# A graph layer's edge network: the constant row of its second layer as two 64-row matmuls, and six gather buffers with a wait every third unit

## The chip, the cores and the metric

The kernel runs on one core of a Trainium2 chip. The metric is the device time of one execution in microseconds (us), taken as the median of several runs. Next to it stands one execution recorded by the hardware profiler; every duration below comes from that one.

## What is computed

One layer of a graph network over 6250 nodes with 256 features and 206250 edges, sorted by destination. Cut to what matters:

```python
h = maximum(layernorm(x), 0)
e = relu(raw @ W_e1.T + b_e1) @ W_e2.T + b_e2        # raw: 64 features of an edge
edge_emb = e * (clip(polarity, 0, 1) + 0.01) @ W_le.T + b_le
msg = relu(h[src] + edge_emb)
aggr = segment_sum(msg, dst, num_segments=6250)
g = (h + aggr) @ W_g1.T + b_g1
out = x + relu(layernorm_affine(g)) @ W_g2.T + b_g2
```

The product of W_e2 and W_le is formed once, so that the edge network has two layers: 64 to 256 with a rectifier, then 256 to 256. The second layer's constant row, c2 = b_e2 @ W_le.T, is added by a matmul of its own.

## The kernel before

The program has three parts, each with lists of instructions written by hand for every engine and joined by semaphores.

**prepare** normalises the nodes and writes h + b_le to a gather table in HBM, while VectorE also splits the weights into a high and a low half (fp32r numbers, of which two stand for one fp32). `fuse` (lines 165 to 176) forms the weights' product and c2; `vector` (from line 184) copies c2 and splits it into rows 0 (high) and 32 (low) of the otherwise zero tile `c2r` (lines 239 to 243). At its end VectorE computes the low halves of the first three units' edge features (`raw_low`, line 405).

**edge_path** goes through 403 units of 512 edges. For unit u:

- GpSimd (lines 530 to 539) issues four indirect DMAs of 128 rows each, which gather h[src] into `hx`, a ring of NX = 4 units. From unit 4 on it waits ahead of each unit's four until VectorE has added the rows of unit u-4 (semaphore `r_t`).
- TensorE has, in this order, the first layer of unit u+1 (lines 675 and 676, four matmuls of 512 columns), the second layer of unit u (lines 685 to 692), and the segment sum of unit u-1 (line 704, four matmuls). Every seventh unit two transposes follow (line 711). The second layer works in two halves q, each in a PSUM bank of its own out of four (`LB`): one matmul of 512 columns with the all-ones tile `onr` and c2, over all 128 array rows (line 685), then twelve of 256 columns.
- ScalarE makes the high halves of the hidden layer (548) and of the messages (554), the one-hot matrices of the destinations (563, 570) and the high half of the features of unit u+3 (400).
- VectorE has, in this order, the low half of the hidden layer of unit u+1 (line 604), for each of four groups of 128 edges the product with the gate plus the gathered row (line 615, in place in the PSUM bank), the low half of the features of unit u+3 (line 405, which reads two tiles of SBUF), and the low half of the messages (line 625). Its wait for a gather stands ahead of each line 615.

Ahead of its second layer TensorE waits for both halves of the hidden layer of unit u; ahead of each bank's first matmul it waits for the low half of the messages of unit u-2 in that bank (`r_ml`).

**node_update** then runs the two last products over the nodes. A fourth part for inputs with crowded destinations exists and is skipped at run time with these inputs.

Of the kernel before, what the change touches and what calls it, by code (L numbers as in the profile page):

```python
# [13 lines left out]
D = 256  # L14
F = 64
# [13 lines left out]
GE = GU * 4 * P  # L29
TOP = NP - P  # L30
NR = 3
NX = 4
NM = 4
AHEAD = 5
FUSE = 8
# [6 lines left out]
def gnn(nc, x, src, dst, src_m, dst_m, pol_m, pol, first, attrT, W_e1T, b_e1, b_e1r, W_e2, b_e2, W_leT, b_le,  # L42
        W_g1T, b_g1, ln_g, ln_b, W_g2T, b_g2, out):
    ctx = ExitStack()
    with ctx:
# [25 lines left out]
        flag_i = sb("flag_i", [1, 1], I32)  # L71
        b1 = sb("b1", [P, 2])
        wc = sb("wc", [P, 2, D])
        c2 = sb("c2", [1, D])
        ble = sb("ble", [P, D])
        lng = sb("lng", [P, 2])
        lnb = sb("lnb", [P, 2])
# [6 lines left out]
        def setup(c):  # L84
# [82 lines left out]
            def fuse(eng):  # L167
                eng.wait_ge(s_w, 16 * len(loads))
                for k in range(2):
                    for m in range(2):  # L170
                        eng.matmul(bank[0][:, D * k:D * k + D], we2[:, m, P * k:P * k + P], wle[:, m, :],
                                   start=(m == 0), stop=(m == 1))
                for m in range(2):
                    last = eng.matmul(bank[1][0:1, 0:D], be2[:, m:m + 1], wle[:, m, :],
                                      start=(m == 0), stop=(m == 1))
                last.then_inc(s_c, 1)

# [5 lines left out]
            def vector(eng):  # L183
                n = [0]

                def link(ins):
                    n[0] += 1
                    ins.then_inc(s_v, 1)
                    eng.wait_ge(s_v, n[0])

                w = 4 * GU
                m = FULL // w
                sv = slot[:, 0:m * w].rearrange("p (g k) -> p g k", k=w)
                bv = base[:, 0:m].rearrange("p (g k) -> p g k", k=1).broadcast_to([P, m, w])
                eng.wait_ge(s_io, 1)
                eng.tensor_copy(iota[:, :], iota_i[:, :])
                eng.memset(low2[:, :], 0.0)
                yield
                eng.wait_ge(s_i, 16 * len(edges))
                eng.tensor_copy(base[:, :], first_i[:, :])  # L200
                link(eng.tensor_copy(slot[:, :], dst_i[:, :]))
                link(eng.tensor_scalar(base[:, :], base[:, :], float(TOP), None, ALU.min))
                yield
                eng.tensor_copy(base_i[:, :], base[0:1, :])
                eng.tensor_tensor(sv, bv, sv, ALU.subtract)
                link(eng.tensor_scalar(slot[:, m * w:TILES], slot[:, m * w:TILES], -1.0, base[:, m:m + 1],
                                       ALU.mult, ALU.add))
                yield
                eng.tensor_reduce(low2[:, 0:1], slot[:, 0:FULL], axis=AX.X, op=ALU.max)
                yield  # L210
                eng.tensor_reduce(low2[:, 1:2], slot[:, 0:FULL], axis=AX.X, op=ALU.min)
                yield
                eng.tensor_copy(low2[0:TAIL, 2:3], slot[0:TAIL, FULL:TILES])
                link(eng.tensor_copy(low2[0:TAIL, 3:4], slot[0:TAIL, FULL:TILES]))
                link(eng.tensor_scalar(low2[:, 0:4:2], low2[:, 0:4:2], 0.0, None, ALU.is_gt))
                link(eng.tensor_scalar(low2[:, 1:4:2], low2[:, 1:4:2], float(1 - P), None, ALU.is_lt))
                eng.tensor_reduce(bad[:, 0:1], low2[:, :], axis=AX.X, op=ALU.max).then_inc(s_bad, 1)
                yield
                eng.wait_ge(s_w, 16 * len(loads))
                eng.wait_ge(s_m, 5)  # L220
                eng.tensor_copy(g1r[0:1, :], bg1[:, :])
                eng.tensor_copy(wgr[:, 0, :, :], wg1[:, :, :])
                link(eng.tensor_copy(wgr[:, 2, :, :], wg2[:, :, :]))
                yield
                eng.tensor_tensor(g1r[32:33, :], bg1[:, :], g1r[0:1, :].bitcast(F32), ALU.subtract)
                eng.tensor_tensor(wgr[:, 1, :, :], wg1[:, :, :], wgr[:, 0, :, :].bitcast(F32), ALU.subtract)
                yield
                eng.tensor_tensor(wgr[:, 3, :, :], wg2[:, :, :], wgr[:, 2, :, :].bitcast(F32), ALU.subtract)
                eng.tensor_copy(w1r[0:F, 0, :], w1[0:F, :])
                eng.tensor_copy(w1r[F:P, 1, :], w1[F:P, :])  # L230
                link(eng.tensor_copy(w1r[0:1, 1, :], btmp[0:1, :]))
                yield
                link(eng.tensor_copy(btmr[32:33, :], btmp[32:33, :]))
                eng.tensor_tensor(w1r[F:P, 0, :], w1[F:P, :], w1r[F:P, 1, :].bitcast(F32), ALU.subtract)
                eng.tensor_tensor(w1r[32:33, 1, :], btmp[32:33, :], btmr[32:33, :].bitcast(F32), ALU.subtract)
                yield
                eng.wait_ge(s_c, 1)
                link(eng.tensor_copy(wc[:, :, :], bank[0][:, :].rearrange("p (k n) -> p k n", k=2)))
                link(eng.tensor_copy(c2[:, :], bank[1][0:1, 0:D]))
                yield  # L240
                eng.tensor_copy(c2r[0:1, :], c2[:, :])
                link(eng.tensor_copy(wcr[:, 0, :, :], wc[:, :, :]))
                eng.tensor_tensor(c2r[32:33, :], c2[:, :], c2r[0:1, :].bitcast(F32), ALU.subtract)
                eng.tensor_tensor(wcr[:, 1, :, :], wc[:, :, :], wcr[:, 0, :, :].bitcast(F32), ALU.subtract)
                yield
                eng.wait_ge(s_f, 1)
                eng.tensor_copy(flag_i[:, :], bank[2][0:1, 0:1])
                yield
# [1 line left out]
            return {"weights": weights, "indices": indices, "gpsimd": gpsimd, "gates": gates, "fuse": fuse, "count_bad": count_bad,  # L250
                    "vector": vector}

        def nodes(c, tag, s_o):
            x_sb = sb(f"x_sb{tag}", [P, NT, D], F32, c)
            h = sb(f"h{tag}", [P, 2, 4, D], F32, c)
            nb = sb(f"nb{tag}", [P, NT], F32, c)
            G = len(NODE_GROUPS)
            s_z = sem(f"s_z{tag}", c)
            s_bl = sem(f"s_bl{tag}", c)
            s_x = [sem(f"s_x{tag}_{i}", c) for i in range(G)]  # L260
            s_st = sem(f"s_st{tag}", c)
            s_ag = sem(f"s_ag{tag}", c)
            s_ep = sem(f"s_ep{tag}", c)
# [27 lines left out]
            def vector(eng):  # L291
                eng.memset(x_sb[96:P, NT - 1, :], 0.0).then_inc(s_z, 1)
                for s in range(G + 1):
                    if s < G:
                        t, n = NODE_GROUPS[s]
                        eng.wait_ge(s_x[s], 16)
                        for k in range(t, t + n):
                            last = eng.bn_stats(st[:, k, :], x_sb[:, k, :])
                        last.then_inc(s_st, 1)
                        eng.wait_ge(s_st, s + 1)  # L300
                        for k in range(t, t + n):
                            last = eng.bn_aggr(mv[:, k, :], st[:, k, :])
                        last.then_inc(s_ag, 1)
                        eng.wait_ge(s_ag, s + 1)
                        eng.tensor_scalar(rs[:, t:t + n], mv[:, t:t + n, 1], EPS, None, ALU.add).then_inc(s_ep, 1)
                    if s >= 1:
                        t, n = NODE_GROUPS[s - 1]
                        eng.wait_ge(s_sq, s)
                        eng.reciprocal(rs[:, t:t + n], rs[:, t:t + n]).then_inc(s_rs, 1)
                        eng.wait_ge(s_rs, s)  # L310
                        eng.scalar_tensor_tensor(out=nb[:, t:t + n], in0=mv[:, t:t + n, 0], scalar=-1.0,
                                                 in1=rs[:, t:t + n], op0=ALU.mult, op1=ALU.mult).then_inc(s_n, 1)
                    yield s
# [93 lines left out]

        def prepare():
            with ExitStack() as c:  # L409
                b = nodes(c, "a", s_oa)  # L410
                a = setup(c)
                block = c.enter_context(nc.Block())

# [44 lines left out]
        def nodes_again():  # L458
            with ExitStack() as c:
                s_ob = sem("s_ob", c)  # L460
                b = nodes(c, "b", s_ob)
                block = c.enter_context(nc.Block())

                @block.sync
# [26 lines left out]
        def edge_path():  # L491
            with ExitStack() as c:
# [37 lines left out]
                def _(eng):  # L530
                    eng.wait_ge(s_oa, 16 * len(NODE_GROUPS))
                    for u in range(UNITS):
                        if u >= NX:
                            eng.wait_ge(r_t, 2 * (u - NX) + 2)
                        for j in range(4):
                            t = 4 * u + j
                            eng.indirect_dma_start(out=hx[:, u % NX, j, :], out_offset=None, in_=tables,  # L537
# [127 lines left out]
                def _(eng):  # L665
# [13 lines left out]
                    def second_layer(u):  # L679
                        eng.wait_ge(r_hh, 2 * u + 2)  # L680
                        eng.wait_ge(r_hl, 2 * u + 2)
                        for q in range(2):
                            if u >= 2:
                                eng.wait_ge(r_ml, 2 * (u - 2) + q + 1)
                            eng.matmul(LB[(2 * u + q) % 4][:, :], onr[:, :], c2w, start=True, stop=False)  # L685
                            for j in range(2):
                                o = LB[(2 * u + q) % 4][:, D * j:D * j + D]
                                e0 = (2 * q + j) * P
# [39 lines left out]
        def general_path(tag):  # L728
            with ExitStack() as c:
# [62 lines left out]
                with nc.Fori(0, NS) as i:  # L792
# [13 lines left out]
                    with nc.Block() as block:  # L806
# [21 lines left out]
                        def _(eng):  # L828
# [4 lines left out]
                            eng.wait_ge(s_hid, 1)  # L833
                            for k in range(2):
                                eng.matmul(bank[2][0:ST, 0:D], hid[:, k, :], wc[:, k, :], start=(k == 0), stop=False)
                            eng.matmul(bank[2][0:ST, 0:D], ones[0:1, 0:ST], c2[:, :], start=False, stop=True).then_inc(s_l2, 1)
                            eng.wait_ge(s_ms, 1)
                            eng.matmul(bank[3][0:ST, 0:D], eq[:, :], msr[:, :], start=True, stop=True).then_inc(s_sum, 1)

# [333 lines left out]
```

## Time and profile before

| | |
|---|---|
| median of 3 runs | 2294.32 us (2292.06 to 2301.87) |
| the profiled execution | 2291.79 us |
| its span, first to last instruction | 2290.1 us |
| TensorE matmul busy | 2220.2 us (97%) |
| VectorE busy | 2143.2 us (94%) |
| ScalarE busy | 1881.2 us (82%) |
| GpSimd busy | 1706.5 us (75%) |
| mean granted TensorE clock | 0.991 |

The span is 1.7 us shorter than the execution. Busy shares are means over stages: prepare lasts to about 72 us, the edge stage to about 2174 us, the node update to the end. GpSimd's busy time leaves out the time between the issue of one gather and the next. Matmuls are pipelined, so that the duration of one reaches beyond the start of the next; the distance from start to start is what one costs in a stream.

### The profile page before, as it was taken

The numbers are of one execution on the slowest core, as the hardware profiler recorded it, in microseconds if no ns is written. First come the engines' busy times: TensorE is split into PE (matmuls) and PEld (weight loads), VectorE is DVE, ScalarE is ACT, GpSimd is POOL, SyncE is SP. The second block draws the span as 40 slices with busy tenths as digits, with TensorE's granted clock in tenths as the row PEclk, the third lists the DMA queues.
The fourth block names the chain that finished last, engine by engine and source line by source line (L and its number), as shares of the span: only waits on it lengthen the run. The fifth ranks groups of instructions, "written<-read, shape, count | busy, mean of one in ns | idle before, by whom it ended". The sixth has DMA issues, their size and how long they took to land. (4 is left out here: it accounts for less than half of the span.)

```text
span 2290.1 us, 45615 instructions
## 1 busy us (share of the span) xinstructions
PE 2220.2 (97%) x14665; PEld 2021.1 (88%) x14665; DVE 2143.2 (94%) x4129; ACT 1881.2 (82%) x4267; POOL 1706.5 (75%) x1671
## 2 busy tenths in 40 slices
PE   3899999999999999999999999999999999999988
PEld 3799999999999999999999999999999999999887
DVE  8899999999999999999999999999999999999888
ACT  6788888888888888888888888888888888888754
POOL 7677777777777777777777777777777777777672
PEclk9899999999999999999999999999999999999989
DMA  9466666666666666666666666666666666666342
GB/s 301 133 158 151 154 152 153 152 153 152 153 152 154 152 153 153 153 153 152 154 151 153 152 152 153 154 152 155 150 154 151 156 150 155 151 153 152 99 132 95
DMA packets 138613, 349.58 MB, mean 153 GB/s; under 512 B 34113, under 2 KB 60674, under 8 KB 138370
## 3 DMA queue, kind: packets, MB, share of 16 engines
q0 software_dynamic: 77376, 211.39, 34.6%
q1 hardware_dynamic: 60994, 135.21, 24.9%
q8 instruction: 121, 1.98, 0.4%
q14 instruction: 122, 1.00, 0.2%
HBM read 333.64 MB, written 12.82 MB: 151 GB/s over the span
## 5 line engine op out<-in xcount | busy, mean ns | idle before, releaser
L537 POOL DMA_INDIRECT hx<-gather_table,sidx x1612 | 1601.7, 994 | 498.5 <-issue 474.1
L691 PE MATMUL bank<-wcr,hh 128*128 128x256 f32 x3224 | 904.6, 281 | 0.0
L690 PE MATMUL bank<-wcr,hh 128*128 128x256 f32 x3224 | 903.3, 280 | 0.0
L692 PE MATMUL bank<-wcr,hl 128*128 128x256 f32 x3224 | 903.2, 280 | 0.0
L615 DVE SCALAR_TENSOR_TENSOR bank<-bank,gt,hx 128x256 f32<-128x256 f32 x1612 | 698.9, 484 | 88.7 <-PE bank L692 86.4
L554 ACT ACTIVATE mhl<-bank 128x512 fp32r<-128x512 f32 x806 | 483.1, 599 | 308.1 <-PE bank L704 187.5
L691 PEld LDWEIGHTS bank<-wcr,hh 128*128 128x128 f32 x3224 | 606.3, 188 | 36.8
L690 PEld LDWEIGHTS bank<-wcr,hh 128*128 128x128 f32 x3224 | 609.2, 189 | 18.1
L692 PEld LDWEIGHTS bank<-wcr,hl 128*128 128x128 f32 x3224 | 605.9, 188 | 0.0
L625 DVE SCALAR_TENSOR_TENSOR mhl<-bank,mhl 128x512 fp32r<-128x512 f32 x806 | 519.2, 686 | 12.6
L604 DVE SCALAR_TENSOR_TENSOR hl<-bank,hh 128x512 fp32r<-128x512 f32 x806 | 514.8, 679 | 4.4 <-ACT hh L548 4.1
L563 ACT ACTIVATE away<-iota,slot 128x128 f32<-128x128 f32 x1612 | 518.1, 401 | 0.0
L548 ACT ACTIVATE hh<-bank 128x512 fp32r<-128x512 f32 x806 | 437.7, 598 | 14.6 <-PE bank L676 8.4
L704 PE MATMUL bank<-mhl,oh 128*128 128x512 f32 x1612 | 443.0, 396 | 1.5 <-DVE mhl L625 1.5
L675 PE MATMUL bank<-rhi,w1r 128*128 128x512 f32 x806 | 322.8, 400 | 7.7 <-PEq L409 7.0
L676 PE MATMUL bank<-rlo,w1r 128*128 128x512 f32 x806 | 320.5, 398 | 0.0
L685 PE MATMUL bank<-c2r,onr 128*128 128x512 f32 x806 | 319.4, 396 | 0.0
L704 PEld LDWEIGHTS bank<-mhl,oh 128*128 128x128 f32 x1612 | 273.1, 188 | 39.9 <-DVE mhl L625 1.9
L405 DVE TENSOR_TENSOR rlo<-raw,rhi 64x512 fp32r<-64x512 f32 x403 | 277.8, 690 | 12.6
L570 ACT ACTIVATE oh<-away 128x512 fp32r<-128x512 f32 x403 | 256.7, 637 | 0.0
L400 ACT CAST rhi<-raw 128x512 fp32r<-128x512 f32 x403 | 250.9, 623 | 0.0
L675 PEld LDWEIGHTS bank<-rhi,w1r 128*128 128x128 f32 x806 | 151.6, 188 | 42.8 <-DVE rlo L405 7.1
(112 smaller groups left out, 1173.4 us busy)
## 6 DMA issues: line engine op xcount, KB each, us to landing
raw<-in_attrT SPq DMA_DIRECT2D x402, 256.0 KB, 4.7
hx<-gather_table,sidx POOLq DMA_INDIRECT x1612, 2.9
x_sba<-in_x SPq DMA_DIRECT2D x12, 512.0 KB, 9.6
gather_table<-x_sba SPq DMA_DIRECT2D x12, 512.0 KB, 6.8
u_x<-in_x SPq DMA_DIRECT2D x12, 512.0 KB, 8.7
out<-u_x SPq DMA_DIRECT2D x12, 512.0 KB
dst_i<-in_dst_m SPq DMA_DIRECT2D x1, 805.5 KB
sidx<-in_src_m SPq DMA_DIRECT2D x1, 805.5 KB
```

The lines of the kernel that those rows point to most:

```text
L537: eng.indirect_dma_start(out=hx[:, u % NX, j, :], out_offset=None, in_=tables, in_offset=bass.IndirectOffsetOnAxis(ap=sidx[:, t:t + 1], ax ...
L548: eng.activation(hh[:, u % 2, k, :], LA[k][:, :], ACT.Relu).then_inc(r_hh, 1)
L554: eng.activation(mh[:, u % 2, 2 * q:2 * q + 2, :], LB[(2 * u + q) % 4][:, :].rearrange("p (j n) -> p j n", j=2), ACT.Relu).then_inc(r_mh, 1)
L563: last = eng.activation(away[:, u % 2, j, :], iota[:, :], ACT.Abs, bias=slot[:, t:t + 1])
L604: eng.scalar_tensor_tensor(out=hl[:, u % 2, k, :], in0=LA[k][:, :], scalar=0.0, in1=hh[:, u % 2, k, :].bitcast(F32), op0=ALU.max, op1=ALU. ...
L615: last = eng.scalar_tensor_tensor(out=b, in0=b, scalar=gt[:, t:t + 1], in1=hx[:, u % NX, 2 * q + j, :], op0=ALU.mult, op1=ALU.add)
L625: eng.scalar_tensor_tensor(out=ml[:, u % 2, 2 * q:2 * q + 2, :], in0=LB[(2 * u + q) % 4][:, :].rearrange("p (j n) -> p j n", j=2), scalar=0.0,
L675: eng.matmul(LA[k][:, :], w1r[:, 0, k * P:k * P + P], rhi[:, u % NM, :], start=True, stop=False)
L690: eng.matmul(o, hh[:, u % 2, k, e0:e0 + P], wcr[:, 0, k, :], start=False, stop=False)
L691: eng.matmul(o, hh[:, u % 2, k, e0:e0 + P], wcr[:, 1, k, :], start=False, stop=False)
L692: last = eng.matmul(o, hl[:, u % 2, k, e0:e0 + P], wcr[:, 0, k, :], start=False, stop=(j == 1 and k == 1))
L704: last = eng.matmul(SG[g % 2][:, :], oh[:, u % 3, j, :], mhl[:, u % 2, j, :, :], start=(u % GU == 0 and j == 0), stop=(ends and j == 3))
```

## The change

c2 is formed in all 128 rows of its tile, and `c2r` holds its halves twice, in rows 0 and 32 and in rows 64 and 96. The constant row of half q is then added by a matmul over array rows 64q to 64q + 63 alone; the two stand next to each other ahead of the 24 others, and the wait for the unit u-2 stands once, for both banks, ahead of them. The gather ring has six units, and GpSimd waits in every third unit, for the adds of unit u-4, which frees the slots of the three units from there on. The semaphores of the nodes' loads are shared by the two node passes, since the larger ring needs more of them.

```diff
-NX = 4
+NX = 6
+NW = 3
-        c2 = sb("c2", [1, D])
+        c2 = sb("c2", [P, D])
@@ fuse
-                    last = eng.matmul(bank[1][0:1, 0:D], be2[:, m:m + 1], wle[:, m, :],
+                    last = eng.matmul(bank[1][:, 0:D], be2[:, m:m + 1].broadcast_to([P, P]), wle[:, m, :],
@@ vector, of prepare
-                link(eng.tensor_copy(c2[:, :], bank[1][0:1, 0:D]))
+                link(eng.tensor_copy(c2[:, :], bank[1][:, 0:D]))
                 yield
-                eng.tensor_copy(c2r[0:1, :], c2[:, :])
+                eng.tensor_copy(c2r[0:1, :], c2[0:1, :])
+                eng.tensor_copy(c2r[F:F + 1, :], c2[F:F + 1, :])
                 link(eng.tensor_copy(wcr[:, 0, :, :], wc[:, :, :]))
-                eng.tensor_tensor(c2r[32:33, :], c2[:, :], c2r[0:1, :].bitcast(F32), ALU.subtract)
+                eng.tensor_tensor(c2r[32:33, :], c2[0:1, :], c2r[0:1, :].bitcast(F32), ALU.subtract)
+                eng.tensor_tensor(c2r[96:97, :], c2[F:F + 1, :], c2r[F:F + 1, :].bitcast(F32), ALU.subtract)
@@ gpsimd, of edge_path
-                        if u >= NX:
-                            eng.wait_ge(r_t, 2 * (u - NX) + 2)
+                        if u >= NX and u % NW == 0:
+                            eng.wait_ge(r_t, 2 * (u + NW - 1 - NX) + 2)
@@ second_layer
                         eng.wait_ge(r_hl, 2 * u + 2)
+                        if u >= 2:
+                            eng.wait_ge(r_ml, 2 * (u - 2) + 2)
                         for q in range(2):
-                            if u >= 2:
-                                eng.wait_ge(r_ml, 2 * (u - 2) + q + 1)
-                            eng.matmul(LB[(2 * u + q) % 4][:, :], onr[:, :], c2w, start=True, stop=False)
+                            eng.matmul(LB[(2 * u + q) % 4][:, :], onr[F * q:F * q + F, :], c2w[F * q:F * q + F],
+                                       start=True, stop=False)
+                        for q in range(2):
                             for j in range(2):
```

## Rows read from the trace of the kernel before

**Rows 1.** Stretch 153:2160; us, PE (x) PEld (x) DVE (x) ACT (x) POOL (x), PEclk, DMA, GB/s

```profile
153.00:2160.00 2007.00, 2007.00 (x13238) 1826.68 (x13237) 1899.90 (x3586) 1708.57 (x3916) 1536.26 (x1545) 1.00 0.61 152
```

**Rows 2.** Waits of that stretch: engine line <- releaser: us in total, times, longest

```profile
POOL hx L537 <- issue: 454.0, 1490, 0.3
...
DVE bank L615 <- PE bank L692: 82.9, 275, 0.5
```

**Rows 3.** Timeline of TensorE, one unit: start us, us, engine line op tiles

```profile
1105.21 0.40 PE L685 MATMUL bank<-c2r,onr 128*128 128x512 f32 x1
1105.45 0.28 PE L690 MATMUL bank<-wcr,hh 128*128 128x256 f32 x1
...
1106.87 0.39 PE L685 MATMUL bank<-c2r,onr 128*128 128x512 f32 x1
...
1110.38 0.40 PE L685 MATMUL bank<-c2r,onr 128*128 128x512 f32 x1
```

**Rows 4.** Timeline of VectorE, one unit and the next

```profile
1003.90 1.68 DVE L615 SCALAR_TENSOR_TENSOR bank<-bank,gt,hx 128x256 f32<-128x256 f32 x4
1005.61 0.69 DVE L405 TENSOR_TENSOR rlo<-raw,rhi 64x512 fp32r<-64x512 f32 x1
...
1008.73 0.87 DVE L615 SCALAR_TENSOR_TENSOR bank<-bank,gt,hx 128x256 f32<-128x256 f32 x2
1009.86 0.88 DVE L615 SCALAR_TENSOR_TENSOR bank<-bank,gt,hx 128x256 f32<-128x256 f32 x2 [0.26 <-PE bank L692]
```

**Rows 5.** Timeline of VectorE and GpSimd: line 405 at 86 us, three gathers

```profile
86.02 0.69 DVE L405 TENSOR_TENSOR rlo<-raw,rhi 64x512 fp32r<-64x512 f32 x1
...
86.17 1.35 POOL L537 DMA_INDIRECT hx<-gather_table,sidx  x1 [0.30 <-issue]
...
92.84 0.95 POOL L537 DMA_INDIRECT hx<-gather_table,sidx  x1 [0.30 <-issue]
...
1006.01 1.11 POOL L537 DMA_INDIRECT hx<-gather_table,sidx  x1 [0.30 <-issue]
```

**Rows 6.** The same at the stage's end: adds of units 400, 402; a gather of 402

```profile
2157.92 1.68 DVE L615 SCALAR_TENSOR_TENSOR bank<-bank,gt,hx 128x256 f32<-128x256 f32 x4
...
2167.01 0.89 DVE L615 SCALAR_TENSOR_TENSOR bank<-bank,gt,hx 128x256 f32<-128x256 f32 x2
...
2160.04 0.95 POOL L537 DMA_INDIRECT hx<-gather_table,sidx  x1 [0.30 <-issue]
```

**Rows 7.** Setup: timeline of VectorE, and a wait of TensorE's weight loads

```profile
67.99 0.41 DVE L243 TENSOR_TENSOR c2r<-c,c2r 1x256 fp32r<-1x256 f32 x1
...
PEld bank L675 <- DVE rlo L405: 7.1, 1, 7.1
```

**Rows 8.** Timeline of TensorE (PE, weight loads PEld) in setup, lines 171, 174, 366

```profile
51.03 0.59 PE L171 MATMUL bank<-wle,we 128*128 128x256 f32 x2
51.24 0.38 PE L171 MATMUL bank<-wle,we 128*128 128x256 f32 x1
51.55 0.38 PE L174 MATMUL bank<-wle,be 128*1 128x256 f32 x1
...
51.55 0.09 PEld L174 LDWEIGHTS bank<-wle,be 128*1 128x1 f32 x2 [0.33 <-issue]
...
52.20 0.38 PE L174 MATMUL bank<-wle,be 128*1 128x256 f32 x1
52.51 0.33 PE L366 MATMUL bank<-ident,ha 128*128 128x128 f32 x1
...
52.67 0.49 PE L366 MATMUL bank<-ident,ha 128*128 128x128 f32 x3
```

**Rows 9.** Timeline of TensorE at 2170 us, behind a stall

```profile
2170.72 0.50 PE L704 MATMUL bank<-mhl,oh 128*128 128x512 f32 x1 [1.48 <-DVE mhl L625]
...
2171.05 0.40 PE L704 MATMUL bank<-mhl,oh 128*128 128x512 f32 x1
```

**Rows 10.** From a gather's issue (line 537) to its landing

```profile
DMA to landing us min/median/max: 2.7/2.9/5.9
```

More of the change, by code:

```diff
@@ L251, in setup, with nodes @@
                     "vector": vector}
-        def nodes(c, tag, s_o):
+        s_x = [sem(f"s_x{i}") for i in range(len(NODE_GROUPS))]
+        def nodes(c, tag, s_o, again):
             x_sb = sb(f"x_sb{tag}", [P, NT, D], F32, c)
@@ L259, in nodes @@
             s_bl = sem(f"s_bl{tag}", c)
-            s_x = [sem(f"s_x{tag}_{i}", c) for i in range(G)]
             s_st = sem(f"s_st{tag}", c)
@@ L295, in vector @@
                         t, n = NODE_GROUPS[s]
-                        eng.wait_ge(s_x[s], 16)
+                        eng.wait_ge(s_x[s], 16 * (again + 1))
                         for k in range(t, t + n):
@@ L409, in prepare @@
             with ExitStack() as c:
-                b = nodes(c, "a", s_oa)
+                b = nodes(c, "a", s_oa, 0)
                 a = setup(c)
@@ L460, in nodes_again @@
                 s_ob = sem("s_ob", c)
-                b = nodes(c, "b", s_ob)
+                b = nodes(c, "b", s_ob, 1)
                 block = c.enter_context(nc.Block())
@@ L835, in _ @@
                                 eng.matmul(bank[2][0:ST, 0:D], hid[:, k, :], wc[:, k, :], start=(k == 0), stop=False)
-                            eng.matmul(bank[2][0:ST, 0:D], ones[0:1, 0:ST], c2[:, :], start=False, stop=True).then_inc(s_l2, 1)
+                            eng.matmul(bank[2][0:ST, 0:D], ones[0:1, 0:ST], c2[0:1, :], start=False, stop=True).then_inc(s_l2, 1)
                             eng.wait_ge(s_ms, 1)
```

## The prediction

> **What bounds the kernel now.** I read the profile from coarse to fine: busy time by stage, then who waits for whom inside the long stage, then one unit of that stage on each engine's timeline. Nearly all of the run is the edge stage, 403 units of 512 edges. From 153 to 2160 us, well inside it, TensorE is busy for all of 2007.00 us at a granted clock of 1.00, which is the 2.4 GHz level [rows 1]. VectorE, in contrast, waits for TensorE's last product of a half unit (line 692) 275 times, 82.9 us in all [rows 2]. So TensorE bounds the stage. One unit lasts 5.17 us from constant-row matmul to constant-row matmul (1105.21 to 1110.38), and each constant-row matmul takes a slot of 0.235 us, start to next start (1105.21 to 1105.45), two a unit: 0.47 us [rows 3]. Matmul durations overlap, so I count starts, never durations.
>
> The other two engines are close. VectorE needs 4.83 us for a unit in which it waits for nothing (1003.90 to 1008.73), and otherwise waits some 0.26 us for TensorE (1009.86) [rows 4]; the window additions of every seventh unit come on top of the 4.83. GpSimd's idle time in the stage is nearly all the issue ahead of each gather, 454.0 us in 1490 pieces, 0.30 each [rows 2]. Without disturbance a gather takes 0.95 us, with its issue 1.25, so 5.00 us a unit (92.84) [rows 5]. Yet the first gather of unit 180, at 1006.01, took 1.11. It looks like the cost of its wait; it isn't. At 92.84 stands the first gather that has such a wait at all (unit 4), and it took 0.95 [rows 5]. And the wait is satisfied long before: the last unit's gathers, from 2160.04 on, wait for the adds of unit 398, while VectorE's adds of unit 400 had begun at 2157.92 and those of unit 402 came at 2167.01 [rows 6]. What stretches the gather is VectorE's subtraction of line 405. At 1005.61 it starts, runs 0.69, and ends 0.29 after the gather's start [rows 4, 5]; the stretch is 0.16. At 86.02 it started just before the gather of 86.17, a gather without any wait; it ended 0.54 after that start, and the gather took 1.35, a stretch of 0.40 [rows 5]. Both fit one rule worked out from these rows: a gather that starts under line 405 is held until about 0.13 us before that much of it would be over, so stretch = end of line 405 after the gather's start, less 0.13. In the last unit, where line 405 no longer runs, the gather is 0.95 again [rows 6]. GpSimd is the faster engine and leans on VectorE's line 405 each unit, which slows it to TensorE's pace.
>
> **The change, part by part.**
>
> *Six buffers, a wait every third unit.* The wait holds nothing now, so removing two of three is worth 0, and the wait that stays asks for the adds of unit u-4, as today. No one is queued behind it but the gathers. It could gain only where GpSimd is ahead by four units; it is about two ahead [rows 6]. Bounds 0 to 0.
>
> *Setup.* One cast and one subtraction of 1x256 are added to VectorE's list. The subtraction took 0.41 us, and TensorE's first edge matmul waits for VectorE's last line 405 of the setup, so the two lie on the path [rows 7]: at most 0.41 each, about 0.7 us together. The bias product over 128 columns in place of one, and the copy of 128 rows in place of one, hide beside them (TensorE idles 7.1 us there). Sharing the load semaphores costs nothing.
>
> *The moved wait.* Both banks' wait for the low half of unit u-2 now stands ahead of the pair. VectorE writes that half before the hidden low half of unit u, for which TensorE waits at the same place, so it is always over: 0.
>
> *The constant rows.* Removed: 2 slots, 0.47 us a unit [rows 3]. Added: two matmuls of 64 rows into two banks. If they run together they take one slot, 0.235, and the unit would shrink by 0.235. But the array's tiling changes before them and again behind them, 806 times in all. No row shows a split by rows; the nearest is the setup's bias product, whose one output column makes it a column split (128*1). There matmuls follow each other every 0.21 us (51.03 and its second, 51.24), and the first of the other shape comes at 51.55, 0.31 after: 0.10 us of nothing, with its weights loaded only then instead of a matmul ahead. Going back, 52.20 to 52.51 is again 0.31: 0.10 more, and the next matmul comes at 52.67, 0.16 later where its peers are 0.11 apart (0.49 less 0.27, halved): 0.05 of weight load uncovered [rows 8]. For this stage's type the uncovered load is the restart after a stall at 2170.72: the next starts at 2171.05, 0.33, where a slot is 0.235: 0.10 [rows 9].
>
> I take: in 0.10 + 0.10, the pair 0.235, out 0.10 + 0.10. The second matmul's weights can be loaded only once the mode is entered, so it starts 0 to 0.10 after the first; no row shows two loads into different rows, and I take the middle, 0.05. Sum 0.685, against 0.47 removed: +0.215 us a unit, x 403 = +86.6. Bounds: both loads at 0.05 and no stagger give 0.535, +26 us; the stagger in full, +107 us; loads wholly hidden, 0.435, -14 us.
>
> The Trainium skill, TensorEngine Tiling (Array Packing), Key Properties, says that changing the tiling mode drains the engine while changing only the tile does not. It gives no price; the trace agrees for a column split (0.10 us each way), and no run here yet shows a row split. The Trainium skill, TensorE: Matmul & The Clock Gate, Part 3, has matmuls in different row groups start some 4 ns apart; by that the stagger would be nil and the sum +66 us.
>
> Against the profiled execution: 2291.79 + 86.6 + 0.7 = 2379. The median of the runs shown is 2.5 us above that execution; I put the forecast at **2380**. TensorE still bounds: VectorE's 4.83 and GpSimd's 5.00 lie under the new 5.4, and GpSimd goes on leaning on line 405, with a longer stretch. The likeliest case's own range is 2320 to 2400.
>
> **The rivals.**
>
> *B, faster: the rows split without a drain.* Then the pair costs 0.235 and TensorE needs 4.93 a unit. The mean unit now is (2160.04 - 92.84) / 398 = 5.194 us [rows 5, 6]; minus 0.235 it would be 4.96. But GpSimd needs 5.00, so it is late next: at best 403 x 0.19 = -77 us, 2216. It can be braked further: with its lead used up, VectorE's fourth add waits for a landing 2.9 us after the gather's start [rows 10], line 405 starts about 0.55 later (an estimate: one add, of which four take 1.68 with overlap [rows 4], and the starts), 3.45 after that gather, which is 0.30 before a start of a later gather at 3 x 1.25 = 3.75; it ends 0.39 into that gather and stretches it by 0.26, a unit of 5.26. Before the lead is gone the collisions are few. Between 5.00 and 5.26 I take 5.08: 403 x 0.115 = -46, so 2249. For it: matmuls of like tiling do flow without gaps. Against it: every change of shape in the trace shows the gap [rows 8].
>
> *C, the brake in full.* As B, but the unit settles at 5.19 to 5.26: 2292 to 2320; the pair's gain ends at GpSimd. The landing of 2.7 to 5.9 us [rows 10] decides the phase.
>
> *D, no pairing and no drain:* the two still take 0.47, 2293 to 2295. The change would not do what it says.
>
> *E, drain and no pairing:* 0.87 against 0.47, +0.40 a unit, +161 us, 2455.
>
> **How the numbers follow.** My case (drain, pair together) 0.54, B 0.27, C 0.06, D 0.05, E 0.08. Within 0.5% (2283 to 2306), which is about what a measurement of this kernel can tell from no change, lie D, half of C and a little of my case's low end; faster by more are B but for its slow edge, and the case of hidden loads. That gives faster 0.28, same 0.11, slower 0.61. The range has to reach B: 2235 to 2410 leaves out E, the top of my case and B's best, under 0.2 together.
>
> **What would show it.** Right: behind the first layer's last matmul of each unit about 0.1 us of nothing on TensorE, the two constant-row weight loads starting only then, the two matmuls nearly at one time, a second gap before line 690's first; a unit of 5.35 to 5.45; VectorE's waits for TensorE doubled; first gathers of some 1.3 us. B: no such gaps, TensorE idle for VectorE, VectorE idle for gathers landing, and GpSimd's gathers back to 0.95. E: the two matmuls 0.235 apart. Wrong on the buffers, if GpSimd's pace changes where TensorE's does not. What would make the sum wrong above all is a row split that the array takes without stopping, or weight loads that go ahead of the change of mode.

## The result, and the profile after

The kernel after takes 2353.62 us (median of four runs, 2351.43 to 2362.55), the kernel before 2293.34 us in its four runs beside it: a ratio of 1.026, with an interval of 1.0225 to 1.0299. The kernel is 60 us slower. The profiled execution took 2351.43 us, with a span of 2349.7, against 2291.79 and 2290.1 before.

The page's busy row, and the same stretch of the edge stage as in [rows 1]:

```profile
PE 2277.7 (97%) x14665; PEld 1906.8 (81%) x14665; DVE 2160.9 (92%) x4131; ACT 1879.5 (80%) x4267; POOL 1730.3 (74%) x1671
```

```profile
153.00:2160.00 2007.00, 2007.00 (x12881) 1671.47 (x12880) 1863.49 (x3489) 1660.40 (x3810) 1523.66 (x1510) 1.00 0.59 149
```

TensorE is still busy for all of the 2007.00 us, at the same granted clock of 1.00, yet in that time it starts 12881 matmuls where it started 13238. So the loss lies inside TensorE's own stream, and the busy share doesn't show it: a gap between two starts counts as busy as long as the duration of the earlier matmul reaches over it.

TensorE's timeline, one stretch around the second layer's start, and the weight loads of the last four rows' time (start us, us, engine, line, operation, tiles). Line 680 is the first layer's last product (676 before), 689 the constant rows (685), 696 and 697 the first two products of the second layer (690, 691), 710 the segment sum (704):

```profile
1102.92 0.50 PE L689 MATMUL bank<-c2r,onr 64*128 64x512 f32 x2
...
1103.58 0.28 PE L697 MATMUL bank<-wcr,hh 128*128 128x256 f32 x1
...
1106.27 1.09 PE L710 MATMUL bank<-mhl,oh 128*128 128x512 f32 x4
...
1107.90 0.40 PE L680 MATMUL bank<-rlo,w1r 128*128 128x512 f32 x1
1108.23 0.50 PE L689 MATMUL bank<-c2r,onr 64*128 64x512 f32 x2
1108.66 0.39 PE L696 MATMUL bank<-wcr,hh 128*128 128x256 f32 x1
1108.89 0.28 PE L697 MATMUL bank<-wcr,hh 128*128 128x256 f32 x1
```

```profile
1107.68 0.19 PEld L680 LDWEIGHTS bank<-rlo,w1r 128*128 128x128 f32 x1
1108.23 0.18 PEld L689 LDWEIGHTS bank<-c2r,onr 64*128 64x128 f32 x2 [0.37 <-issue]
1108.66 0.19 PEld L696 LDWEIGHTS bank<-wcr,hh 128*128 128x128 f32 x1 [0.25 <-issue]
1108.77 0.19 PEld L697 LDWEIGHTS bank<-wcr,hh 128*128 128x128 f32 x1
```

The reader is to see three things. The two constant-row matmuls stand as one row ("x2") of 0.50 us, that is, at one time. From line 680 to them pass 0.33 us, where [rows 3] have 0.235 for a slot; from them to line 696 pass 0.43, and from there to 697 0.23, where 0.12 is the rule. And the weight loads of 689 and of 696 start only at the recorded starts of their own matmuls (1108.23 and 1108.66), while that of 697 starts 0.12 ahead of its matmul, as loads do elsewhere in the unit. The unit lasts from 1102.92 to 1108.23: 5.31 us, against 5.17.

Who waits for whom, whole span (engine, tile and line, what it waits for: us in total, times, longest):

```profile
POOL hx L541 <- issue: 454.9, 1493, 0.3
...
PEld bank L689 <- issue: 147.5, 403, 0.7
DVE bank L619 <- PE bank L698: 124.8, 290, 1.3
...
PEld bank L696 <- issue: 99.3, 403, 0.4
...
POOL hx L541 <- DVE bank L619: 60.0, 118, 1.2
```

The two weight loads that stand still do so 403 times each, once a unit: that is the change, counted.

From the starts of all units without transposes, the medians are:

| slot | before, us | after, us |
|---|---|---|
| first layer's last product to the constant row | 0.232 | 0.327 |
| constant row to the second layer's first product | 0.238 and 0.230 (two a unit) | 0.430 behind the second of the pair, which starts 0.003 behind the first |
| first product to the second | 0.120 | 0.224 |
| whole unit | 5.167 | 5.313 |

With the transposes of every seventh unit the mean unit is 5.199 before and 5.345 after. From the first unit's constant row to the last one's pass 2088.75 us before and 2147.11 after: 58.4 of the 59.6 us by which the spans differ. Another 0.97 lies ahead of the first constant row (76.10 before, 77.07 after; see Setup below), and 0.3 behind the last.

### The profile page after: what moved, and what is told of

It is laid out like the page before. It is cut to its first block and busy times, and to the rows that moved or that the text cites. A ratio compares the mean times of both kernels' runs of the same rounds, so it can differ in the third digit from the quotient of the medians.

```text
span 2349.7 us, 45617 instructions
## 1 busy us (share of the span) xinstructions
PE 2277.7 (97%) x14665; PEld 1906.8 (81%) x14665; DVE 2160.9 (92%) x4131; ACT 1879.5 (80%) x4267; POOL 1730.3 (74%) x1671
## 5 line engine op out<-in xcount | busy, mean ns | idle before, releaser
L541 POOL DMA_INDIRECT hx<-gather_table,sidx x1612 | 1625.4, 1008 | 523.4 <-issue 454.9
L696 PE MATMUL bank<-wcr,hh 128*128 128x256 f32 x3224 | 944.9, 293 | 0.0
L697 PE MATMUL bank<-wcr,hh 128*128 128x256 f32 x3224 | 901.1, 279 | 0.0
L619 DVE SCALAR_TENSOR_TENSOR bank<-bank,gt,hx 128x256 f32<-128x256 f32 x1612 | 708.8, 485 | 130.5 <-PE bank L698 124.8
L689 PE MATMUL bank<-c2r,onr 64*128 64x512 f32 x806 | 202.6, 496 | 0.0
L689 PEld LDWEIGHTS bank<-c2r,onr 64*128 64x128 f32 x806 | 75.1, 183 | 147.5 <-issue 147.5
```

Source lines behind the costliest of these rows:

```text
L619: last = eng.scalar_tensor_tensor(out=b, in0=b, scalar=gt[:, t:t + 1], in1=hx[:, u % NX, 2 * q + j, :], op0=ALU.mult, op1=ALU.add)
L696: eng.matmul(o, hh[:, u % 2, k, e0:e0 + P], wcr[:, 0, k, :], start=False, stop=False)
L697: eng.matmul(o, hh[:, u % 2, k, e0:e0 + P], wcr[:, 1, k, :], start=False, stop=False)
```

## The experiments

They ran later, on three chips on which the kernel before itself takes 2819, 2773 and 2762 us: there VectorE sees the gathered rows late (experiments 3, 4 and 7). The chip of the result above is not on record; it is called the first chip here. A total that depends on gathers is therefore compared only within one chip; TensorE's slots in undisturbed units are the same on all of them. In all kernels the line numbers move by a few.

### 1. Do the two matmuls run together, and by their rows? (e3_same_rows)

```diff
-  eng.matmul(LB[...], onr[F * q:F * q + F, :], c2w[F * q:F * q + F], start=True, stop=False)
+  eng.matmul(LB[...], onr[0:F, :], c2w[0:F], start=True, stop=False)
```

> The changed kernel, but both constant-row matmuls use array rows 0 to 63, into their two banks. Theory (in the changed kernel the two run together): one slot of 0.235 us more a unit, 403 x 0.235 = +95 us on 2353, so 2448, with the two matmuls 0.235 apart and perhaps the second's weight load on top. Rival (they never ran together; the records' 4 ns are modelled): 2353.

TensorE's timeline:

```profile
1013.95 0.40 PE L680 MATMUL bank<-rlo,w1r 128*128 128x512 f32 x1
1014.27 0.73 PE L689 MATMUL bank<-c2r,onr 64*128 64x512 f32 x2
1014.93 0.39 PE L696 MATMUL bank<-wcr,hh 128*128 128x256 f32 x1
1015.15 0.28 PE L697 MATMUL bank<-wcr,hh 128*128 128x256 f32 x1
```

The way in (0.32) and the way out (0.22 behind 696) are those of the kernel after; the pair to 696 takes 0.66 instead of 0.43. The second matmul now starts 0.334 us after the first (the median, like the next figures): read with the kernel after, a slot of 0.235 and the load of about 0.10 on the way in, which falls between the two starts here. To 696 it is 0.323 instead of 0.430, so that over all the constant rows cost 0.224 us a unit more, one slot: a second 64-row matmul behind the first, with no change of tiling between them, costs no more than a slot. So in the kernel after the two do run at one time, and it is the difference of rows that lets them; that the records only model it is ruled out by the 0.224. The total, 3397.95 us in one run, is set by the late gathers and says nothing here.

### 2. What does one round trip between the tilings cost? (e4_own_places)

```diff
                         for q in range(2):
                             eng.matmul(LB[...], onr[F * q:F * q + F, :], c2w[F * q:F * q + F], start=True, stop=False)
-                        for q in range(2):
                             for j in range(2):
```

> The changed kernel, but each 64-row matmul stands ahead of its own bank's twelve products, as in the kernel before, so that the tiling changes four times a unit and nothing runs together. Theory (each change costs 0.095 us of nothing and 0.104 of uncovered weight load): the two slots of 0.47 stay, and 4 x 0.20 = 0.80 us a unit come on top of the kernel before: 2293 + 321 = 2614 us. Rival (the loss comes from the two being adjacent, or is paid once a unit): 2353 plus one slot, 2448, or less.

TensorE's timeline:

```profile
1004.05 0.40 PE L680 MATMUL bank<-rlo,w1r 128*128 128x512 f32 x1
1004.38 0.49 PE L689 MATMUL bank<-c2r,onr 64*128 64x512 f32 x1
1004.80 0.38 PE L695 MATMUL bank<-wcr,hh 128*128 128x256 f32 x1
1005.02 0.28 PE L696 MATMUL bank<-wcr,hh 128*128 128x256 f32 x1
...
1006.19 0.28 PE L697 MATMUL bank<-wcr,hl 128*128 128x256 f32 x1
1006.40 0.50 PE L689 MATMUL bank<-c2r,onr 64*128 64x512 f32 x1
1006.83 0.39 PE L695 MATMUL bank<-wcr,hh 128*128 128x256 f32 x1
```

An undisturbed unit lasts 5.940 us, 0.773 above the kernel before: 0.39 for each round trip, close to the 0.80 expected for both. The numbers of its parts: 0.327 - 0.232 = 0.095 into the 64-row tiling behind a product of 512 columns, and 0.208 - 0.117 = 0.091 behind one of 256 (1006.19 to 1006.40 in the rows). One such matmul alone takes 0.421 or 0.428 to the next product, the pair of the kernel after 0.430: the second of the pair is free, and nearly all of the 0.43 is what one would cost. The total, 3412.49 us in one run, is again that of the late gathers and can't be set against the 2614 expected.

### 3. The rows alone, and the buffers alone (e2_rows_only, e1_buffers_only)

e2 is the kernel after with the old ring:

```diff
-NX = 6
-NW = 3
+NX = 4
-                        if u >= NX and u % NW == 0:
-                            eng.wait_ge(r_t, 2 * (u + NW - 1 - NX) + 2)
+                        if u >= NX:
+                            eng.wait_ge(r_t, 2 * (u - NX) + 2)
```

> The changed kernel with four gather buffers and the wait in every unit, as before. Theory (the whole loss is the two 64-row matmuls): the time of the changed kernel, 2353 us within 0.5%. Rival (the buffers hide a part of the loss or add to it): away from 2353 by more than 12 us.

e1 is the kernel before with the reverse of this edit, and the shared load semaphores.

> The kernel before with six gather buffers and a wait in every third unit, nothing else. Theory (the wait never holds a gather; VectorE's line 405 stretches it): the time of before, 2293 us within 0.5%, and the first gather of nearly every unit still takes some 1.11 us, also in the two units of three that have no wait. Rival (the wait itself costs GpSimd the 0.16 us): the units without a wait show 0.95 us in all four gathers, and only every third unit 1.11.

Measured: e2 2822.55 us against 2818.78 for the kernel before on that chip, 1.0018 (1.0006 to 1.0029); e1 3382.17, 1.199 (1.197 to 1.201). Both have to be read with the waits. Those of e2:

```profile
POOL hx L540 <- DVE bank L618: 578.0, 200, 5.7
...
DVE bank L618 <- remote: 180.8, 74, 7.2
```

and of e1:

```profile
POOL hx L539 <- DVE bank L617: 1143.6, 133, 11.1
...
DVE bank L617 <- remote: 1020.8, 196, 14.8
```

"Remote" is the landing of a gather. On this chip GpSimd and VectorE wait for each other's rows in both kernels, and TensorE is busy for 85% of the span in e2 and 81% in e1: it bounds neither, and its longer unit is hidden in e2, whose slots are those of the kernel after (0.327, 0.003, 0.428, 0.224). e2 is inconclusive on the total. e1 was expected to change nothing, and it costs a fifth there. GpSimd's timeline in e1:

```profile
1629.70 1.27 POOL L539 DMA_INDIRECT hx<-gather_table,sidx  x1 [8.15 <-DVE bank L617]
...
1643.79 0.94 POOL L539 DMA_INDIRECT hx<-gather_table,sidx  x1 [0.30 <-issue]
1653.37 1.27 POOL L539 DMA_INDIRECT hx<-gather_table,sidx  x1 [8.63 <-DVE bank L617]
```

Twelve gathers, three units, go out in one run from 1629.70 to 1644.73, and then GpSimd stands still for 8.63 us until the adds that its one wait asks for. A cycle of three units lasts 23.67 us, 7.89 a unit. With the ring of four the waits come 200 times, every second unit, and take 578.0 / 200 = 2.9 us each.

### 4. The buffers once more, on a third chip (e9_buffers_again)

The same kernel as e1.

> The same kernel as e1_buffers_only once more: in the first run the kernel before itself took 2819 us on that chip, with gathers that VectorE saw land over 20 us after their issue. Where the kernel before takes 2293 us, theory: 2293 us within 0.5%, first gathers of nearly every unit 1.11 us, with a wait or without. Rival (the wait costs GpSimd the 0.16 us): 0.95 us in the units without a wait. Where gathers land late again: slower by some 20% as in the first run, since GpSimd then stops for three units' worth of adds at a time instead of one's.

```profile
POOL hx L539 <- DVE bank L617: 1063.5, 133, 10.7
```

3311.0 us against 2773.02, 1.195 (1.192 to 1.198): again 133 waits, 8.0 us each, and again a kernel before that is far above its first 2293. This is the expectation's last case, gathers that land late again; its first, the ring where the kernel before takes 2293 us, stays untested by itself. It is no oddity of one chip; what sets these chips apart from the first is not settled.

### 5. One constant row in place of two (e5_one_row, e6_one_row_buffers)

```diff
-  eng.matmul(LB[...], onr[:, :], c2w, start=True, stop=False)
+  if q == 0:
+      eng.matmul(LB[...], onr[:, :], c2w, start=True, stop=False)
```

The first products of the other bank open it instead. This gives TensorE what an ideal pair would give, with no change of tiling.

> The kernel before with the second bank's constant-row matmul left out (its first product opens the bank instead), all in 128 rows: TensorE gets the slot that an ideal pair would give back, with no change of tiling. The constant is missing from half of the messages. Rival B of the prediction: GpSimd is late next; a unit of 5.00 to 5.19, likeliest 5.08, 2216 to 2292 us, about 2249. Rival C: braked in full by line 405, 2292 to 2320. If TensorE stays the bound with no brake: 403 x 0.235 = 95 us less, 2198.

> As the run with one constant row left out, plus six gather buffers and a wait in every third unit. Theory (GpSimd lags by its pace and by line 405, never by the wait): the same time as with four buffers, within 0.5%. Rival (the wait costs 0.16 us each time, or the ring is full): faster by 0.107 x 403 = 43 us or so.

The kernel e6 is e5 with the ring of six. e5: 2819.09 against 2819.31, 0.9998 (0.9985 to 1.0012). e6: 3380.78, 1.197 (1.193 to 1.201). e6 was expected at the time of e5 and is a fifth slower, as e1 is above the kernel before. Both totals are those of the gathers on this chip, like e2 and e1, so neither tells whether GpSimd would have held up a faster TensorE on the first one. Inconclusive.

### 6. Does VectorE's line 405 hold the gathers? (e7_one_row_short_low, e8_short_low)

```diff
-  eng.tensor_tensor(rlo[F:P, u % NM, :], part(u)[F:P], rhi[F:P, u % NM, :].bitcast(F32), ...
+  w = 512 if u < NM else 2
+  eng.tensor_tensor(rlo[F:P, u % NM, 0:w], part(u)[F:P, 0:w], rhi[F:P, u % NM, 0:w].bitcast(F32), ...
```

> As the run with one constant row left out, and VectorE's line 405 cut to 2 of its 512 columns from unit 4 on (the low half of the edge features is then stale). Theory (line 405 holds the gathers): every gather 0.95 us, GpSimd at 5.00 us a unit; with TensorE at 4.96 the stage goes at 5.00 to 5.02: 2215 to 2225 us. Rival (the gathers are slowed by something else, such as their waits): first gathers stay above 1.05 us, and the time that of the run with one row left out.

> The kernel before with VectorE's line 405 cut to 2 of its 512 columns from unit 4 on (the low half of the edge features is then stale). Theory (GpSimd leans on line 405, TensorE bounds): the time of before, 2293 us within 0.5%, gathers at 0.95 us from the start, and GpSimd running ahead until its ring of four is full; only then does the wait hold the first gather of a unit. Rival (GpSimd or VectorE bounds the kernel before): faster, down to 2230.

e8 is the kernel before with this edit, e7 is e5 with it. All gathers of one kernel, durations in ns (shortest/median/longest), of e2, which has the whole line 405, and then of e8:

```profile
L540 POOL DMA_INDIRECT hx<-gather_table,sidx x1612: 945/949/1280, 73.0 to 2681.5; - x180
```

```profile
L538 POOL DMA_INDIRECT hx<-gather_table,sidx x1612: 940/946/1189, 72.2 to 2717.0; - x180
```

With the line cut to two columns the mean gather is 0.946 us instead of 0.993, and the longest, 1.189, is the very first. In the kernel before, 389 gathers start while line 405 runs; the prediction's rule (what is left of the line, less 0.13 us) gives 73.7 us of stretch for them, and 75.4 are measured, with none on the other 1223. So the holder is line 405, and the rule stands for gathers that start 0.1 us or more behind the line's start, as all of these do; it fails for those that start right with it (Six buffers, below). The totals do not bear on it, and both miss what was expected (2215 to 2225, and 2293 us): e7 is 1.0009 (0.9993 to 1.0026), e8 1.012 (1.010 to 1.014), slower although VectorE has less to do and no gather is held. Why e8 loses 37 us on a chip where the landings set the time stays open.

### 7. The rows without the gathers (e10, e11, e12)

To get TensorE back as the bound, gathers are issued for the first units only, and VectorE adds the same rows again and again. e10 is the kernel before so cut, e11 the kernel after, e12 is e5.

```diff
-                    for u in range(UNITS):
-                        if u >= NX:
-                            eng.wait_ge(r_t, 2 * (u - NX) + 2)
+                    for u in range(NX):
@@
-                                eng.wait_ge(r_hx[t % (4 * NX)], 16 * (t // (4 * NX) + 1))
+                                eng.wait_ge(r_hx[t % (4 * NX)], 16)
```

> The kernel before with gathers for the first four units alone; later units add the rows that lie in the ring (so the messages have the wrong nodes' rows). It takes the gathers out of the race, since on the last three occasions they landed too late for TensorE to bound. Theory (TensorE bounds the edge stage at 5.19 us a unit): the 2293 us of the first measurement, within 1%. Rival (something beside the gathers slows these chips): above 2400.

> The changed kernel with gathers for the first six units alone, the same part left out. Theory (the whole loss is TensorE's, the two changes of tiling a unit): 403 x 0.146 = +59 us on the kernel before without gathers, 2353 us. Rival (a part of the loss came by way of the gathers or the ring): less than 45 us between the two.

> The kernel before without the second bank's constant-row matmul (half of the messages lack the constant) and with gathers for the first four units alone. It shows what a pair with no change of tiling would give where GpSimd sets no bound. Theory (TensorE bounds down to 4.96 us a unit, VectorE needs 4.83 and its window additions): 403 x 0.235 = 95 us less than the kernel before without gathers, 2198 us. Rival (VectorE, waiting for TensorE inside the unit, bounds earlier): 40 us less or below that.

Measured: e10 2303.02 us (2302.81 to 2313.05), within 1% of 2293 as expected, so that without the gathers this chip is hardly slower than the first; e11 2372.89 (2371.82 to 2374.18), 69.9 above e10 where 59 were expected; e12 2215.3 (2210.41 to 2220.41), 88 below it where 95 were expected. The constant rows from 300 to 2000 us, of e10, e11 and e12 (durations in ns, first and last start):

```profile
L683 PE MATMUL bank<-c2r,onr x655: 392/400/400, 299.6 to 1999.8; 128*128 128x512 f32 x164
```

```profile
L687 PE MATMUL bank<-c2r,onr x638: 491/492/500, 300.1 to 1999.3; 64*128 64x512 f32 x160
```

```profile
L684 PE MATMUL bank<-c2r,onr x342: 394/400/400, 300.1 to 1995.1; 128*128 128x512 f32 x171
```

Per unit: e10 (1999.8 - 299.6) / 327 = 5.199, e11 (1999.3 - 300.1) / 318 = 5.343, e12 (1995.1 - 300.1) / 341 = 4.971. e11 is 0.144 above e10, as after is above before: the whole loss of the edge stage comes again with no gather under way, from TensorE's stream. The totals are 69.9 apart, not 59, because of the start. VectorE's adds of unit 1 in e10, and in e11, each behind the last gather that GpSimd issues:

```profile
91.34 0.95 POOL L535 DMA_INDIRECT hx<-gather_table,sidx  x1 [0.30 <-issue]
...
95.18 1.28 DVE L613 SCALAR_TENSOR_TENSOR bank<-bank,gt,hx 128x256 f32<-128x256 f32 x3 [5.78 <-remote]
```

```profile
102.33 0.95 POOL L539 DMA_INDIRECT hx<-gather_table,sidx  x1 [0.30 <-issue]
...
107.12 1.27 DVE L617 SCALAR_TENSOR_TENSOR bank<-bank,gt,hx 128x256 f32<-128x256 f32 x3 [15.52 <-remote]
```

In e10 sixteen gathers go out in a row, in e11 twenty-four, and both times VectorE sees the rows of unit 1, which were among the first eight, only 3 to 4 us after GpSimd has finished the last: it waits 5.78 us for them in e10 and 15.52 in e11. From the first constant row to the last pass 2099.5 us in e10 and 2167.2 in e11, 67.7 apart; 58.4 of them are the units, and the other 9.3 come near the 9.7 by which that wait is longer. The longer setup accounts for about one more.

In e12 TensorE is busy throughout as well (from 153 to 2080 us without a break), and the mean unit is 0.228 us shorter than in e10, nearly the whole slot; the rival, VectorE bounding earlier, fell. But VectorE is busy for 1897.85 of those 1927 us, so it is next. The 88 us are what an ideal pair would bring where GpSimd holds nothing up.

No kernel here was faster than the kernel before with the whole computation in it.

## Why the prediction was right, and where its size was off

**The time.** 2353.62 us lies 26 below the 2380 forecast, and inside the likeliest case's own range of 2320 to 2400.

**The bound.** Right. TensorE set the unit before and sets it after; VectorE and GpSimd fit into the longer one.

**The constant rows.** The mechanism was the likeliest case's: a gap and a late weight load on each side, and the pair together in one slot. Term by term, per unit:

| term | predicted, us | measured, us |
|---|---|---|
| two slots removed | 0.470 | 0.232 + 0.238 + 0.230 less the 0.232 that stays: 0.468 |
| gap in | 0.10 | 0.327 - 0.232 = 0.095 |
| load in, pair, gap out | 0.10 + 0.235 + 0.10 = 0.435 | 0.430 from the second of the pair |
| stagger of the pair | 0.05 | 0.003 |
| load out uncovered | 0.10 | 0.224 - 0.120 = 0.104 |
| all other slots | 0 | -0.018 |
| sum | +0.215 | +0.146 |

The term that failed is the stagger. The prediction reasoned that the second matmul's weights could be loaded only once the new tiling was entered, and took the middle of 0 and 0.10 for want of a row; the lower end was true, and that is 0.047 x 403 = 19 of the 28 us by which the edge stage was overrated. The gaps and loads were sized well from rows of quite another place, the setup's column split [rows 8] and a restart [rows 9]: 0.095 + (0.430 - 0.235) + 0.104 = 0.394 against 0.40, 2 us together. Some 7 us more lie in slots that the change doesn't touch. The 23 products of 256 columns behind 697 take 1106.27 - 1103.58 = 2.69 us; before, the 24 take 2.83 (1105.45 to 1106.87 [rows 3], and 1107.10 to 1108.51 in the same timeline), less one of 0.12 is 2.71. They run a little closer where no constant row stands between the halves; no run here separates the cause.

The Trainium skill, TensorE: Matmul & The Clock Gate, Part 3, has matmuls in different row groups start some 4 ns apart. The trace agrees, with 3 to 4 ns, and by that rule the sum would have been nearer: the prediction itself gives +66 us for it, where the edge stage grew by 58.4. The Trainium skill, TensorEngine Tiling (Array Packing), Key Properties, has a change of tiling mode drain the engine. The trace agrees for a split by rows as well, with 0.095 us.

**Setup.** Predicted 0.7, at most 0.82; measured 0.84, of which the added cast and the added subtraction take 0.73 from start to next start (0.30 and 0.43); with the first unit's gap in, 0.095, that is nearly all of the 0.97 by which the first constant row starts later. The moved wait was put at 0, and in the stretch of [rows 1] TensorE waits for no low half. VectorE's list, with the added cast and the added subtraction (line 246):

```profile
67.63 0.28 DVE L243 CAST c2r<-c 1x256 fp32r<-1x256 f32 x1
68.39 0.42 DVE L245 TENSOR_TENSOR c2r<-c,c2r 1x256 fp32r<-1x256 f32 x1
68.82 0.42 DVE L246 TENSOR_TENSOR c2r<-c,c2r 1x256 fp32r<-1x256 f32 x1
...
70.02 1.90 DVE L409 TENSOR_TENSOR rlo<-raw,rhi 64x512 fp32r<-64x512 f32 x3
```

The last row, for whose end TensorE waits, started at 69.18 before.

**Six buffers.** Zero was right where it was predicted: 58.4 + 0.97 + 0.3 account for the 59.6, and nothing is left for the buffers; nor is anything hidden by them, since the unit grows by as much without gathers (0.144, experiment 7). The picture of GpSimd, which leans on line 405 and has a first gather of some 1.3 us, held in the main: from unit 65 on, 291 of 338 units have a stretched first gather, of 1.25 us as a rule. That of unit 196, and VectorE's line 409 (405 before):

```profile
1107.64 1.25 POOL L541 DMA_INDIRECT hx<-gather_table,sidx  x1 [0.30 <-issue]
```

```profile
1107.39 0.69 DVE L409 TENSOR_TENSOR rlo<-raw,rhi 64x512 fp32r<-64x512 f32 x1
```

The line ends 0.44 after the gather's start, 0.44 - 0.13 = 0.31, and the stretch is 0.30. What the prediction did not foresee is where its rule ends. In the kernel after, 40 gathers start within 0.05 us behind the line's start. 39 of them are not held at all; the line itself is longer instead, 0.73 to 0.77 us. The first gather of unit 202:

```profile
1139.48 0.76 DVE L409 TENSOR_TENSOR rlo<-raw,rhi 64x512 fp32r<-64x512 f32 x1
```

```profile
1139.52 0.95 POOL L541 DMA_INDIRECT hx<-gather_table,sidx  x1 [0.30 <-issue]
```

Up to unit 64 only about every second unit has a stretched gather, and GpSimd draws ahead of VectorE's adds, from 7.2 us at unit 4 to 16.2 at unit 50 and 19.0 at unit 200, about 3.6 units, where the kernel before stays at some 8 us, 1.5 units. So the prediction's "about two units ahead" didn't hold with the longer unit. From unit 69 on GpSimd reaches the end of the ring:

```profile
1102.31 1.27 POOL L541 DMA_INDIRECT hx<-gather_table,sidx  x1 [0.51 <-DVE bank L619]
```

There are 47 such waits, of 0.50 to 1.17 us with the issue of 0.30 in each, 38.4 us in all. The other 71 of the 118 in the list of waits are the issue alone, 0.30 each, which the profile puts down to VectorE, as it does with 55 in the kernel before. It cost nothing, since a GpSimd that waits at the ring's end is late for no one. What was not foreseen at all is what the same ring costs where landings are seen late (experiments 3 and 4): a fifth of the time. The prediction's "bounds 0 to 0" held on the first chip alone.

**VectorE's waits for TensorE** were to double. In the stretch of [rows 2] they rose from 82.9 to 114.6 us, by two fifths:

```profile
DVE bank L619 <- PE bank L698: 114.6, 268, 0.5
```

The unit grew less than predicted, and VectorE's own busy time per unit rose from 1899.90 / 386.0 = 4.92 to 1863.49 / 375.5 = 4.96 us (the divisors are 2007 us over the mean units).

**The rivals.** D (nothing changes) and E (no pairing) fell by the slots, B and C (no gap) likewise. How far GpSimd would have braked a faster TensorE, which was the price of B and C, stays open: e5 was to show it and could not, and e12 leaves the gathers out.

## What to carry to other kernels

Splitting TensorE's rows between two small matmuls does run them at one time, but it is bought with a round trip between tilings, here 0.40 us, so it pays only where one round trip saves more than that: two slots of 0.235 become one, and the trade is lost by 0.16 in these slots, 0.146 on the whole unit. Count the changes of tiling per unit before counting the saved slots, and put all split matmuls behind one change: with two round trips in place of one the unit of experiment 2 is 0.63 us longer than that of the kernel after, a slot and a round trip. A ring that waits more seldom is free only as long as the producer is early; try it where landings are late before keeping it.

## What the runs showed of the hardware that was not expected

- Weight loads do not go ahead of a change of tiling: each change costs about 0.095 us of gap and then a load of about 0.10 us that elsewhere in the unit hides under the matmul before. Four changes a unit cost 0.773 us, two cost 0.40.
- Two 64-row matmuls on different rows start 0.003 us apart with their weight loads included; on the same rows, 0.334, of which about 0.10 is the load on the way in.
- A gather that starts within 0.05 us behind the start of VectorE's line 409 is not held (39 of 40 in the kernel after); the line takes up to 0.77 us instead of 0.69. One that starts 0.1 us or more behind it is held until about 0.13 us before the line's end.
- On the three later chips VectorE sees gathers late, and at no fixed time behind their issue. In e10 and e11 the rows of unit 1 are seen 2.9 and 3.8 us after GpSimd has finished the last gather of the run (at 95.18 with 16 in a row, at 107.12 with 24), those of unit 0 while it still issues. Where VectorE stands still for rows, it sees them 21 to 24 us after GpSimd has finished their gather in e2, 25 to 35 in e1 and e9; on the first chip 2.7 to 5.9 us pass from issue to landing [rows 10]. The gathers' packets end 2.3 to 4.6 us after the issue on all four alike; what delays the sight of them is open.
